# Subtracting the row maxima in attention with four 32-row tiles of the TensorE array instead of 64-row tiles

## The chip, the cores and the metric

The kernel runs on one core of one Trainium2 chip. The metric is the time of one execution in microseconds (us), as the median of several runs. A profile of one execution goes with it.

## The reference

The program is a transformer block: a layernorm, an attention layer with rotary positions, and a gated feed-forward layer whose inputs are rounded to blockwise FP4. The change is in the attention alone:

```
scores = einsum('bhid,bhjd->bhij', qr, kr) * 64**-0.5
probs  = softmax(scores, axis=-1)
out    = einsum('bhij,bhjd->bhid', probs, v)
```

There are 4 batches of 1024 tokens, 16 heads of 64 channels. The softmax subtracts each query's largest score before the exponential.

## The kernel before

Everything is written out by hand in Bass: one program for each engine, which runs its instructions in order, with semaphores between the engines.

**Tiling.** Two heads make a pair, 8 pairs a batch, 32 pairs (P) in all. Head 0 of a pair lies in partitions 0 to 63, head 1 in 64 to 127. A pair has 16 steps: 2 chunks (c) of 512 queries, each against 8 tiles (jt) of 128 keys. The loop of a pair (`pair(P)`) goes through 8 step pairs d = 0 to 7, each with the steps 2d and 2d+1.

**A step's scores.** `scores` (L853) writes, for each head, the transposed scores of 128 keys by 512 queries to one PSUM bank, `st[step % 2][:, a]`; so two buffers st with two banks each. Queries and keys are split into a high and a low part (`heads`), and the product is made of three terms. A fourth term subtracts the row maxima: the stationary operand `one_rows` has ones in its first four rows of each head, and `max_rows` holds in those rows, for each block of 128 queries, the negated maxima and zeros elsewhere. Each term is a pair of matmuls with 64 rows, one for each head, in the two halves of the array. A step waits until the exponential of the step two before it has read its st.

**Exponential.** ScalarE (L449) turns each st (128x1024) into `probs`, a ring of 8. TensorE multiplies probs by v into `po` (L865, 128 rows by 64 columns of the array, `times_v`), one step pair behind the scores.

**Row maxima.** They are those of the high parts alone, for the pair that comes next. `max_scores` (L898) writes 128 queries by 512 keys of both heads to `mx`, of which there is one buffer; VectorE reduces it to `negmax` (L644, `row_maxima`) and only then may the next mx be written. Each step pair has two such units, one ahead of its scores and one behind. After eight of them VectorE gathers `maxcol` (L649), TensorE transposes it (L905, `max_transpose`, unit "B", at the end of d=2 and d=6) and VectorE spreads it, times `mask`, over `max_rows` (L658). `mask` is 1 where the row of a head belongs to the block of queries.

**The other work of a step pair** goes through one PSUM bank, `ms`: the projections of keys and queries (L888, unit "K", d=0 to 3, read by VectorE in L674 and L675), of v (L878, "V", d=4 and 5), the output projection (L923, "O", d=6 and 7), and the sums of the probabilities over the keys (L914, "S", 128 rows by 32 columns, d=1 and 5). VectorE also adds the first two tiles of probs (L666, `first_sum`) at d=1, 3, 5 and 6; GpSimd adds the rest.

**TensorE's order in a step pair** is thus: first mx, scores of step 2d, scores of step 2d+1, second mx, the K, V or O unit, po of the two steps before, and the B or S unit if there is one. Pairs 0 to 30 have mx in all step pairs; pair 31 has it at d=0 and d=1 only.

Of the kernel before, what the change touches and what calls it, by code (L numbers as in the profile page):

```python
# [8 lines left out]
F32 = mybir.dt.float32  # L9
F32R = mybir.dt.float32r  # L10
I32 = mybir.dt.int32
ALU = mybir.AluOpType
ACT = mybir.ActivationFunctionType
AX = mybir.AxisListType
# [3 lines left out]
HEADS, HD = 16, 64  # L18
# [9 lines left out]
JT = TOKENS // PART  # L28
CH = 512
RING = 8  # L30
STEPS = 2 * JT
HALF = TPB // 2
SETS = 3
FIRST_KEYS = 2
QUARTER = CH // 2
KSL = [(0, 128), (128, 128), (256, FFN - 256)]
GT = 4
# [8 lines left out]
def wait(engine, semaphore, value):  # L46

    if value > 0:
        engine.wait_ge(semaphore, value)
# [7 lines left out]
def block_program(nc, ctx, x_d, gamma_d, beta_d, wqkv_d, wout_d, bout_d, wg_d, wu_d, wd_d,  # L57
                  cos_d, sin_d, ident_d, sums_d, recips_d, out_d):
    def sb(name, shape, dt=F32):
        return ctx.enter_context(nc.sbuf_tensor(name, shape, dt))  # L60

    def sem(name):
        return ctx.enter_context(nc.semaphore(name))
# [6 lines left out]
    ident = sb("ident", [PART, PART])  # L70
# [14 lines left out]
    max_rows = sb("max_rows", [PART, TOKENS], F32R)  # L85
    one_rows = sb("one_rows", [PART, PART], F32R)
    mask = sb("mask", [PART, HALF])
    v = sb("v", [PART, 2, JT, PART])
    negmax = sb("negmax", [PART, 2, 2, HALF, 2])
    maxcol = sb("maxcol", [PART, 2, PART])  # L90
    probs = sb("probs", [PART, RING, 2, CH])
    first_sum = sb("first_sum", [PART, 2, 2, CH])
    psum_keys = sb("psum_keys", [PART, 2, 2, CH])
    sums = sb("sums_kept", [PART, 2, QUARTER])
    oT = sb("oT", [PART, 2, TOKENS])
# [34 lines left out]
    st = [ctx.enter_context(nc.psum_tensor(f"st{i}", [PART, 2, CH], F32)) for i in range(2)]  # L130
# [9 lines left out]
    const_done, one_rows_done = sem("const_done"), sem("one_rows_done")  # L140
# [8 lines left out]
    mask_done, key_part = sem("mask_done"), sem("key_part")  # L149
    maxcol_done = sem("maxcol_done")  # L150
    st_ps, exp_done, pv_ps, key_sum = sem("st_ps"), sem("exp_done"), sem("pv_ps"), sem("key_sum")
# [19 lines left out]
    def maxima_at(P, d, second):  # L171

        n = 2 * d + second - 4
        return (P + 1, n) if n >= 0 else (P, n + 16)
# [9 lines left out]
    def units_at(P, d):  # L184

        return [(kind, target(P, kind, u), u) for kind, u in UNITS[d] if 0 <= target(P, kind, u) < PAIRS]
# [5 lines left out]
    def read_out(engine, unit):  # L192

        engine.wait_ge(ms_free, order_of[unit] + 1)

    def keys_added(P, c):

        return (JT - FIRST_KEYS - 1) * (2 * P + c)

# [16 lines left out]
    def present(P):  # L216

        return 0 <= P < PAIRS
# [90 lines left out]
    def _(pool):  # L309
# [3 lines left out]
        nc.gpsimd.memset(w_raw[:, :], 0.0).then_inc(const_done, 1)  # L313

        pool.wait_ge(const_done, 1)
        for a in range(2):
            nc.gpsimd.memset(one_rows[HD * a:HD * a + HALF, :].bitcast(F32), 1.0).then_inc(one_rows_done, 1)
        pool.wait_ge(one_rows_done, 2)

        def add_step(P, i):  # L320
            c, jt = i // JT, i % JT
            if jt <= FIRST_KEYS:
                return
            wait(pool, exp_done, STEPS * P + i + 1)
            if jt == FIRST_KEYS + 1:
                if P > 0:
                    filled(pool, ("S", P - 1, c))
                first = probs[:, (STEPS * P + i - 1) % RING]
            else:
                pool.wait_ge(key_sum, keys_added(P, c) + jt - FIRST_KEYS - 1)  # L330
                first = psum_keys[:, c]
# [82 lines left out]
    def _(act):  # L414
# [24 lines left out]
        def exp(P, i):  # L439
            step_n = STEPS * P + i  # L440
            act.wait_ge(st_ps, step_n + 1)
            if step_n >= RING:
                act.wait_ge(pv_ps, step_n - RING + 1)
                old, c, jt = (step_n - RING) // STEPS, ((step_n - RING) // JT) % 2, (step_n - RING) % JT
                if jt < FIRST_KEYS:
                    act.wait_ge(key_part, 2 * (2 * old + c) + 2)
                else:
                    act.wait_ge(key_sum, keys_added(old, c) + max(jt - FIRST_KEYS, 1))
            nc.scalar.activation(probs[:, step_n % RING], st[step_n % 2][:, :], ACT.Exp, scale=SCALE)\  # L449
# [8 lines left out]
        def sum_copy(F, c):  # L458
            filled(act, ("S", F, c))
            wait(act, sums_out, 16 * (2 * F + c - 1))  # L460
            nc.scalar.activation(sums[:, c, :], ms[:, 0:QUARTER], ACT.Copy).then_inc(ms_free, 1)  # L461

# [72 lines left out]
    def _(dve):  # L535
# [86 lines left out]
        mean_and_rstd(ln_attention, TPB, TILES, True)  # L622
        normalise_x(TPB, TILES)
        dve.wait_ge(consts_in, 96)
        nc.vector.tensor_tensor(mask[:, :], ident[:, 0:HALF], ident[:, HD:HD + HALF], ALU.add).then_inc(mask_done, 1)
        dve.wait_ge(mask_done, 1)

        def quantise_weights():
# [17 lines left out]

        def max_columns(N, c):
            dve.wait_ge(mx_free, 16 * N + 8 * c + 8)
            nc.vector.tensor_reduce(maxcol[:, c].rearrange("p (a k) -> p a k", a=2)[:, :, 0:HALF], negmax[:, c], AX.X,  # L649
                                    ALU.min).then_inc(maxcol_done, 1)  # L650

        def spread_maxima(N, c):

# [145 lines left out]
    def _(pe):  # L799
        mm = nc.tensor.matmul  # L800
        pe.wait_ge(consts_in, 96)
        pe.wait_ge(const_done, 1)
        pe.wait_ge(one_rows_done, 2)
        def transpose_xn(b):
            for c in range(2):
                pe.wait_ge(xn_done, TPB * b + 4 * c + 4)
                wait(pe, xnT_done, 2 * b + c - 1)
                for t in range(4):
                    last = nc.tensor.transpose(halves[c][:, t * PART:(t + 1) * PART],
                                               xn[:, b * TPB + 4 * c + t, :],  # L810
                                               ident[:, :])
                last.then_inc(xnT_ps, 1)
# [22 lines left out]
        def bank(unit):  # L835

            wait(pe, ms_free, order_of[unit])

        def scores(P, i):
            c, jt, step_n = i // JT, i % JT, STEPS * P + i  # L840
            if i == 0:
                pe.wait_ge(lo_done, 2 * P + 2)
            if jt == 0:
                read_out(pe, ("B", P, c))
            wait(pe, exp_done, step_n - 1)
            (k_hi, k_lo), (q_hi, q_lo) = ([heads[:, P % SETS, s, part] for part in range(2)] for s in range(2))
            keys, queries = bass.ts(jt, PART), bass.ts(c, CH)
            terms = ((k_lo[:, keys], q_hi[:, queries]), (k_hi[:, keys], q_hi[:, queries]),
                     (k_hi[:, keys], q_lo[:, queries]), (one_rows[:, :], max_rows[:, queries]))
            for n, (stationary, moving) in enumerate(terms):  # L850
                for a in range(2):
                    rows = slice(HD * a, HD * a + HD)
                    last = mm(st[step_n % 2][:, a], stationary[rows], moving[rows], start=(n == 0), stop=(n == 3))  # L853
            last.then_inc(st_ps, 1)

        def times_v(step_n):
# [34 lines left out]
        def max_scores(N, u):  # L891
            t, half = u // 2, u % 2
            wait(pe, mx_free, 16 * N + u)
            if u == 0:
                pe.wait_ge(hi_done, 2 * N + 2)
            for a in range(2):
                rows = slice(HD * a, HD * a + HD)
                last = mm(mx[:, a, :], heads[rows, N % SETS, 1, 0, bass.ts(t, PART)],  # L898
                          heads[rows, N % SETS, 0, 0, bass.ts(half, CH)], start=True, stop=True)
            last.then_inc(mx_full, 1)  # L900

        def max_transpose(N, c):
            bank(("B", N, c))
            pe.wait_ge(maxcol_done, 2 * N + c + 1)
            nc.tensor.transpose(ms[:, 0:PART], maxcol[:, c, :], ident[:, :]).then_inc(ms_full, 1)  # L905

        def softmax_sums(F, c):
# [3 lines left out]
            for part in (first_sum, psum_keys):  # L911
                for j in range(4):
                    a, quarter = j // 2, bass.ts(j % 2, QUARTER)
                    last = mm(ms[32 * j:32 * j + 32, 0:QUARTER], ones[:, 0:32], part[:, c, a, quarter],  # L914
                              start=part is first_sum, stop=part is psum_keys)
# [10 lines left out]

        def pair(P):
            for d in range(JT):
                N, u = maxima_at(P, d, 0)
                if present(N):  # L930
                    max_scores(N, u)
                if present(P):
                    scores(P, 2 * d)
                    scores(P, 2 * d + 1)
                N, u = maxima_at(P, d, 1)
                if present(N):
                    max_scores(N, u)
                for kind, X, u in units_at(P, d):
                    if kind == "K":
                        project_kq(X, u)  # L940
                    if kind == "V":
                        project_v(X, u)
                    if kind == "O":
                        output_projection(X, u)
                for n in (STEPS * P + 2 * d - 2, STEPS * P + 2 * d - 1):
                    if 0 <= n < STEPS * PAIRS:
                        times_v(n)
                for kind, X, u in units_at(P, d):
                    if kind == "B":
                        max_transpose(X, u)  # L950
                    if kind == "S":
                        softmax_sums(X, u)
# [106 lines left out]
```

## Time and profile before

| | |
|---|---|
| median of 3 runs | 1789.6 us (1787.51 to 1791.94) |
| profiled execution | 1791.84 us |
| span of its profile | 1790.1 us |
| mean granted TensorE clock | 0.962 |
| TensorE matmuls busy | 1613.1 us (90%) |
| VectorE / ScalarE / GpSimd busy | 1217.2 / 701.8 / 1234.8 us |

The span goes from the first to the last instruction in the profile; PE is TensorE's matmuls and PEld its weight loads, which overlap them; DVE is VectorE, ACT ScalarE, POOL GpSimd. The recorded duration of a matmul covers its passage through the array, and matmuls overlap: what one costs in a row of them is the distance between starts. Two matmuls in different row groups of the array run side by side.

### The profile page before, as it was taken

What the parts mean: (1) busy time and instruction counts of PE and PEld (TensorE: products, weight loads), DVE (VectorE), ACT (ScalarE), POOL (GpSimd) and SP (SyncE); (2) the same over time, 40 slices, a digit from 0 to 9 for tenths busy, and PEclk for the clock granted to TensorE, in tenths of its full rate; (3) what the DMA queues carried; (4) which work ended last, traced back from release to release, by engine and by line L of the source; (5) the groups of instructions that cost most, each with busy time, mean ns of one, the idle gap of its engine ahead of it and who ended that gap; (6) DMA issues with size and microseconds to landing.
All of it is one profiled execution on the core that took longest, in us unless ns stands there. A gap on an engine that the chain in (4) does not pass through costs nothing.

```text
span 1790.1 us, 25976 instructions
## 1 busy us (share of the span) xinstructions
PE 1613.1 (90%) x10025; PEld 872.1 (49%) x10025; DVE 1217.2 (68%) x1589; ACT 701.8 (39%) x885; POOL 1234.8 (69%) x562
## 2 busy tenths in 40 slices
PE   2499999999999999999999999999999999962576
PEld 1245555555555555555555555555555555531355
DVE  6566666666666666666666666676666666657787
ACT  0134444444444444444444444444444444421122
POOL 1647777777777777777777777777777777551563
PEclk9789999999999999999999999999999999985788
DMA  3111111111111111111111111111111111000000
GB/s 106 35 33 43 38 41 29 39 43 42 42 32 42 42 43 43 41 37 42 43 43 43 42 40 40 38 31 41 43 42 35 38 42 38 15 15 7 6 18 24
DMA packets 69194, 67.12 MB, mean 37 GB/s; under 512 B 26512, under 2 KB 52432, under 8 KB 69072
## 3 DMA queue, kind: packets, MB, share of 16 engines
q1 hardware_dynamic: 69072, 65.46, 14.3%
q8 instruction: 80, 1.31, 0.3%
q14 instruction: 42, 0.34, 0.1%
HBM read 29.25 MB, written 2.62 MB: 18 GB/s over the span
## 4 chain that ended last, share of the span: by engine, by line
PE 81%; DVE 15%; POOL 2%; issue 1%; DMA 0%; ACT 0%; SPq 0%; DVEq 0%; POOLq 0%
PE po L865 26%; PE st L853 23%; PE mx L898 9%; PE ms L888 8%; PE ms L878 4%; PE ms L923 4%; PE ms L914 4%; DVE negmax L644 2%; DVE first_sum L666 2%; DVE max_rows L658 1%; PE ms L905 1%; DVE amax L588 1%; DVE kq L720 1%; PE st L1000 1%; PE mx L977 1%
## 5 line engine op out<-in xcount | busy, mean ns | idle before, releaser
L644 DVE TENSOR_REDUCE negmax<-mx 128x2 f32<-128x1024 f32 x512 | 625.6, 1222 | 417.6 <-PE mx L898 417.6
L449 ACT ACTIVATE probs<-st 128x1024 f32<-128x1024 f32 x512 | 498.0, 1024 | 574.0 <-PE st L853 574.0
L332 POOL TENSOR_TENSOR psum_keys<-psum_keys,probs 128x1024 f32<-128x1024 f32 x256 | 607.5, 2373 | 149.7 <-ACT probs L449 132.7
L865 PE MATMUL po<-probs,v 128*64 128x512 f32 x2048 | 495.7, 605 | 0.0
L853 PE MATMUL st<-heads 64*128 64x512 f32 x3072 | 440.0, 391 | 0.0
L853 PEld LDWEIGHTS st<-heads 64*128 64x128 f32 x3072 | 289.9, 185 | 58.6 <-issue 2.4
L898 PE MATMUL mx<-heads 64*128 64x512 f32 x1024 | 236.7, 458 | 42.6 <-DVE negmax L644 41.9
L865 PEld LDWEIGHTS po<-probs,v 128*64 128x64 f32 x2048 | 124.3, 136 | 256.1 <-issue 147.1
L332 POOL TENSOR_TENSOR psum_keys<-probs 128x1024 f32<-128x1024 f32 x64 | 151.6, 2369 | 121.1 <-ACT probs L449 121.1
L344 POOL TENSOR_TENSOR kq<-kq 128x1024 f32<-128x1024 f32 x64 | 152.2, 2378 | 76.6 <-DMA kq<-sin_part 76.6
L853 PE MATMUL st<-max_rows,one_rows 64*128 64x512 f32 x1024 | 202.0, 389 | 0.0
L898 PEld LDWEIGHTS mx<-heads 64*128 64x128 f32 x1024 | 97.2, 186 | 211.0 <-issue 124.5
L888 PE MATMUL ms<-xnT,wqkv 128*128 128x512 f32 x256 | 151.1, 673 | 19.6 <-DVE sin_part L675 17.5
L666 DVE TENSOR_REDUCE first_sum<-probs 128x512 f32<-128x1024 f32 x128 | 159.3, 1245 | 5.1 <-ACT probs L449 5.1
L339 POOL TENSOR_TENSOR oT<-oT,rsum 128x512 f32<-128x512 f32 x64 | 82.3, 1286 | 111.4 <-DMA rsum<-recips 111.2
L348 POOL TENSOR_TENSOR heads<-kq,heads 128x1024 fp32r<-128x1024 f32 x64 | 153.1, 2393 | 1.6 <-ACT heads L472 1.6
L853 PEld LDWEIGHTS st<-max_rows,one_rows 64*128 64x128 f32 x1024 | 96.9, 185 | 21.7
L674 DVE TENSOR_TENSOR kq<-ms,cos 128x512 f32<-128x512 f32 x128 | 87.6, 684 | 23.0 <-PE ms L888 15.9
L923 PE MATMUL ms<-wout,oT 128*128 128x128 f32 x512 | 75.9, 292 | 22.6 <-issue 20.7
L658 DVE TENSOR_TENSOR max_rows<-ms,mask 128x512 fp32r<-128x512 f32 x64 | 44.3, 692 | 70.6 <-PE ms L905 70.6
L675 DVE TENSOR_TENSOR sin_part<-ms,sin 128x512 f32<-128x512 f32 x128 | 87.2, 681 | 0.0
L461 ACT ACTIVATE sums_kept<-ms 128x256 f32<-128x256 f32 x64 | 24.6, 385 | 153.4 <-PE ms L914 153.4
(129 smaller groups left out, 1145.1 us busy)
## 6 DMA issues: line engine op xcount, KB each, us to landing
kq<-sin_part SPq DMA_DIRECT2D x256, 128.0 KB, 2.4
rsum<-recips SPq DMA_DIRECT2D x128, 128.0 KB, 2.9
wqkv<-in_L_attn_w_qkv_dram SPq DMA_DIRECT2D x32, 192.0 KB, 2.7
resid<-in_L_attn_x_dram SPq DMA_DIRECT2D x4, 512.0 KB, 6.1
wout<-in_L_attn_w_out_dram SPq DMA_DIRECT2D x32, 64.0 KB, 2.6
out_dram<-resid SPq DMA_DIRECT2D x8, 256.0 KB, 2.3
sums<-sums_kept SPq DMA_DIRECT2D x64, 4.0 KB
spread<-sums SPq DMA_DIRECT2D x64, 4.0 KB, 1.6
```

Source lines behind the costliest of these rows:

```text
L332: nc.gpsimd.tensor_tensor(psum_keys[:, c], first, probs[:, (STEPS * P + i) % RING], ALU.add)\
L344: nc.gpsimd.tensor_tensor(raw[s], raw[s], swp[s], ALU.add).then_inc(rotated, 1)
L348: nc.gpsimd.tensor_tensor(heads[:, L % SETS, s, 1], raw[s], heads[:, L % SETS, s, 0].bitcast(F32), ALU.subtract)\
L449: nc.scalar.activation(probs[:, step_n % RING], st[step_n % 2][:, :], ACT.Exp, scale=SCALE)\
L644: nc.vector.tensor_reduce(negmax[:, t // HALF, :, t % HALF, half], mx[:, :], AX.X, ALU.max, negate=True)\
L666: nc.vector.tensor_reduce(first_sum[:, c, a], probs[:, 0:FIRST_KEYS, a].rearrange("p r n -> p n r"), AX.X, ALU.add).then_inc(key_part, 1)
L674: nc.vector.tensor_tensor(raw[s][:, columns], ms[:, :], cos[:, columns], ALU.mult).then_inc(cos_done, 1)
L853: last = mm(st[step_n % 2][:, a], stationary[rows], moving[rows], start=(n == 0), stop=(n == 3))
L865: last = mm(po[HD * a:HD * a + HD, :], v[:, P % 2, jt, HD * a:HD * a + HD], probs[:, step_n % RING, a], start=(jt == 0), stop=(jt == JT - 1))
L888: mm(ms[:, :], wqkv[:, L % 2, 1 - s, :], batch(L)[:, bass.ts(c, CH)], start=True, stop=True)\
L898: last = mm(mx[:, a, :], heads[rows, N % SETS, 1, 0, bass.ts(t, PART)], heads[rows, N % SETS, 0, 0, bass.ts(half, CH)], start=True, stop=True)
L923: last = mm(ms[:, bass.ts(t, D)], oT[:, F % 2, bass.ts(HALF * u + t, PART)], wout[:, :], start=True, stop=True)
```

## The change

The term with the row maxima leaves `scores` and becomes the function `minus_maxima`, called once for a step pair, ahead of the first mx. It makes four matmuls of 32 rows each, in four row tiles of the array, one for each of the two steps and two heads, into the four st banks. They open the accumulation (`start=True`), and the three terms of `scores` add to it. `max_rows` and `one_rows` therefore hold each head's rows twice (partitions 0, 32, 64 and 96 on), `maxcol` is written by two reductions, and `mask` sums four blocks of the identity. The wait for st moves along: the four matmuls wait for the exponentials of both steps of the step pair before, and at the first tile of a chunk for `max_rows`.

```
+        for j in range(4):
+            nc.gpsimd.memset(one_rows[QUAD * j:QUAD * j + HALF, :].bitcast(F32), 1.0).then_inc(one_rows_done, 1)
...
+        nc.vector.tensor_reduce(mask[:, :], ident[:, :].rearrange("p (j q) -> p q j", j=4)[:, 0:HALF], AX.X, ALU.add)\
...
-            nc.vector.tensor_reduce(maxcol[:, c].rearrange("p (a k) -> p a k", a=2)[:, :, 0:HALF], negmax[:, c], AX.X,
-                                    ALU.min).then_inc(maxcol_done, 1)
+            for twin in range(2):
+                nc.vector.tensor_reduce(maxcol[:, c].rearrange("p (s a k) -> p s a k", s=2, a=2)[:, twin, :, 0:HALF],
+                                        negmax[:, c], AX.X, ALU.min).then_inc(maxcol_done, 1)
...
+        def minus_maxima(P, i):
+            c, step_n = i // JT, STEPS * P + i
+            if i % JT == 0:
+                read_out(pe, ("B", P, c))
+            wait(pe, exp_done, step_n)
+            for j in range(4):
+                rows = slice(QUAD * j, QUAD * j + QUAD)
+                mm(st[j // 2][:, j % 2], one_rows[rows, :], max_rows[rows, bass.ts(c, CH)], start=True, stop=False,
+                   tile_position=(QUAD * j, 0))
+
         def scores(P, i):
             c, jt, step_n = i // JT, i % JT, STEPS * P + i
             if i == 0:
                 pe.wait_ge(lo_done, 2 * P + 2)
-            if jt == 0:
-                read_out(pe, ("B", P, c))
-            wait(pe, exp_done, step_n - 1)
...
-                     (k_hi[:, keys], q_lo[:, queries]), (one_rows[:, :], max_rows[:, queries]))
+                     (k_hi[:, keys], q_lo[:, queries]))
...
-                    last = mm(st[step_n % 2][:, a], stationary[rows], moving[rows], start=(n == 0), stop=(n == 3))
+                    last = mm(st[step_n % 2][:, a], stationary[rows], moving[rows], start=False, stop=(n == 2))
...
-            pe.wait_ge(maxcol_done, 2 * N + c + 1)
+            pe.wait_ge(maxcol_done, 2 * (2 * N + c) + 2)
...
         def pair(P):
             for d in range(JT):
+                if present(P):
+                    minus_maxima(P, 2 * d)
```

## Rows read from the trace of the kernel before

**Rows 1.** The page: busy time of each engine, and the chain that ended last.
```profile
PE 1613.1 (90%) x10025; PEld 872.1 (49%) x10025; DVE 1217.2 (68%) x1589; ACT 701.8 (39%) x885; POOL 1234.8 (69%) x562
...
PE 81%; DVE 15%; POOL 2%; issue 1%; DMA 0%; ACT 0%; SPq 0%; DVEq 0%; POOLq 0%
```

**Rows 2.** Stretch with attention: length, busy us (instructions) by engine, clock, DMA.
```profile
126.00:1640.00 1514.00, 1451.06 (x9354) 768.81 (x9352) 1014.27 (x1212) 643.92 (x756) 1106.56 (x500) 0.99 0.15 38
```

**Rows 3.** Timeline of TensorE's matmuls, one step pair (d=1): start us, length us, instructions.
```profile
668.29 0.50 PE L898 MATMUL mx<-heads 64*128 64x512 f32 x2
668.63 0.86 PE L853 MATMUL st<-heads 64*128 64x512 f32 x6
669.33 0.39 PE L853 MATMUL st<-max_rows,one_rows 64*128 64x512 f32 x2
...
670.25 0.40 PE L853 MATMUL st<-max_rows,one_rows 64*128 64x512 f32 x2
670.49 0.40 PE L898 MATMUL mx<-heads 64*128 64x512 f32 x2
670.81 1.12 PE L888 MATMUL ms<-xnT,wqkv 128*128 128x512 f32 x2
671.87 1.94 PE L865 MATMUL po<-probs,v 128*64 128x512 f32 x8
673.74 0.64 PE L914 MATMUL ms<-first_sum,ones 128*32 128x256 f32 x8
...
674.74 0.50 PE L898 MATMUL mx<-heads 64*128 64x512 f32 x2
```

**Rows 4.** Timeline of the weight loads at the end of it (idle before, releaser).
```profile
673.74 0.16 PEld L914 LDWEIGHTS ms<-first_sum,ones 128*32 128x32 f32 x8 [0.81 <-DVE sin_part L675]
...
674.74 0.19 PEld L898 LDWEIGHTS mx<-heads 64*128 64x128 f32 x2 [0.41 <-issue]
674.84 0.65 PEld L853 LDWEIGHTS st<-heads 64*128 64x128 f32 x6
```

**Rows 5.** Timeline of all engines, from the end of d=6 to d=7.
```profile
703.22 0.33 PE L905 MATMUL ms<-ident,maxcol 128*128 128x128 f32 x1
...
703.48 0.51 PE L898 MATMUL mx<-heads 64*128 64x512 f32 x2
...
703.59 0.69 DVE L658 TENSOR_TENSOR max_rows<-ms,mask 128x512 fp32r<-128x512 f32 x1 [1.39 <-PE ms L905]
...
704.20 1.25 DVE L666 TENSOR_REDUCE first_sum<-probs 128x512 f32<-128x1024 f32 x1
...
705.37 1.21 DVE L644 TENSOR_REDUCE negmax<-mx 128x2 f32<-128x1024 f32 x1
...
706.63 0.19 PEld L898 LDWEIGHTS mx<-heads 64*128 64x128 f32 x2 [1.24 <-DVE negmax L644]
...
707.07 0.41 PEld L923 LDWEIGHTS ms<-wout,oT 128*128 128x128 f32 x3 [0.25 <-issue]
```

**Rows 6.** Timeline of VectorE in the step pair of rows 3.
```profile
668.83 1.23 DVE L644 TENSOR_REDUCE negmax<-mx 128x2 f32<-128x1024 f32 x1 [0.93 <-PE mx L898]
...
672.19 0.17 DVE L649 TENSOR_REDUCE maxcol<-negmax 128x8 f32<-128x16 f32 x1
672.30 0.69 DVE L674 TENSOR_TENSOR kq<-ms,cos 128x512 f32<-128x512 f32 x1
672.90 0.68 DVE L675 TENSOR_TENSOR sin_part<-ms,sin 128x512 f32<-128x512 f32 x1
```

**Rows 7.** Waits over the span: us in total, times, longest us.
```profile
PEld mx L898 <- DVE negmax L644: 66.6, 47, 8.6
```

**Rows 8.** Timeline at the start of d=4: the first mx and its reduction.
```profile
685.85 0.50 PE L898 MATMUL mx<-heads 64*128 64x512 f32 x2
...
686.63 1.17 DVE L644 TENSOR_REDUCE negmax<-mx 128x2 f32<-128x1024 f32 x1
```

**Rows 9.** Timeline of ScalarE in the step pair of rows 3.
```profile
669.76 1.95 ACT L449 ACTIVATE probs<-st 128x1024 f32<-128x1024 f32 x2 [0.75 <-PE st L853]
```

More of the change, by code:

```diff
@@ L34 @@
 FIRST_KEYS = 2
+QUAD = 32
 QUARTER = CH // 2
@@ L315, in _ @@
         pool.wait_ge(const_done, 1)
-        for a in range(2):
-            nc.gpsimd.memset(one_rows[HD * a:HD * a + HALF, :].bitcast(F32), 1.0).then_inc(one_rows_done, 1)
-        pool.wait_ge(one_rows_done, 2)
+        for j in range(4):
+            nc.gpsimd.memset(one_rows[QUAD * j:QUAD * j + HALF, :].bitcast(F32), 1.0).then_inc(one_rows_done, 1)
+        pool.wait_ge(one_rows_done, 4)
         def add_step(P, i):
@@ L624, in _ @@
         dve.wait_ge(consts_in, 96)
-        nc.vector.tensor_tensor(mask[:, :], ident[:, 0:HALF], ident[:, HD:HD + HALF], ALU.add).then_inc(mask_done, 1)
+        nc.vector.tensor_reduce(mask[:, :], ident[:, :].rearrange("p (j q) -> p q j", j=4)[:, 0:HALF], AX.X, ALU.add)\
+          .then_inc(mask_done, 1)
         dve.wait_ge(mask_done, 1)
@@ L802, in _ @@
         pe.wait_ge(const_done, 1)
-        pe.wait_ge(one_rows_done, 2)
+        pe.wait_ge(one_rows_done, 4)
         def transpose_xn(b):
```

## The prediction

> **What bounds the kernel now.** I read the page's busy times first [rows 1]: TensorE's matmuls fill 90% of the span, VectorE 68%, ScalarE 39%, GpSimd 69%. The chain that ended last agrees, 81% TensorE and 15% VectorE. The stretches [rows 2] say where: from 126 to 1640 us, which is nearly all of the attention, matmuls cover 1451.06 of 1514 us at the full clock (0.99). So a microsecond taken off TensorE's queue counts there, unless VectorE turns out to stand right behind it. That needs one step pair at close range.
>
> The timeline of TensorE shows one step pair, d=1, whole [rows 3]. Pairs of 64-row products that follow each other start 0.23 us apart: the eight of two steps run from 668.63 to 670.49, 1.86 us. Where the shape of the array tile changes, it is dearer. The first pair of mx starts at 668.29 and the next pair only at 668.63, 0.34 instead of 0.23. The weight-load rows [rows 4] say why. Inside one shape the next weights load while the last products stream (674.84, 0.10 after the mx products start at 674.74). After a change of shape the loads begin only when the stream before is through: the idle of 0.41 us ahead of the mx loads at 674.74 is such a change, and the products then have to wait for those loads. The purest case is in [rows 5]: the mx pair at 706.63 came as the first and last of its shape, and the next shape's loads start at 707.07, 0.44 later.
>
> VectorE must reduce the first mx before the second may be written, for there is one mx buffer. In [rows 6] the first reduction starts at 668.83, takes 1.23 and ends at 670.06. How soon TensorE could go on after that is in [rows 5]: reduction 705.37 + 1.21 = 706.58, loads at 706.63, so 0.05. Second mx's loads might thus start at 670.11; the products start at 670.49, so the loads start 0.23 ahead of them, at 670.26. The slack is 0.15 us. This is the row the whole forecast rests on. The waits say the same from the other side: TensorE's mx loads waited for a reduction 47 times in 512 [rows 7].
>
> **The change part by part.**
>
> *Taken away:* in each pair of steps the two max_rows pairs (669.33 and 670.25 in [rows 3]), 2 x 0.23 = 0.46 us. Both lie between the first and the second mx. There are 32 x 8 = 256 step pairs.
>
> *What of that arrives.* With 0.46 gone the second mx meets VectorE. First mx to start of reduction 668.83 - 668.29 = 0.54, reduction 1.23, release 0.05, and then the mx pair loads and streams by itself, 0.44 to the next shape: 2.26 us from first mx to the ms unit. Before it is 670.81 - 668.29 = 2.52. So only 0.26 of the 0.46 arrives; the rest turns into a wait for VectorE.
>
> *Added:* one group of four 32-row products, ahead of the first mx. No row of before shows 32-row tiles. The price has two parts. The group itself: four column tiles of 32 run side by side (eight products of L914 with 256 columns in 0.64 us, [rows 3]) and their loads too (eight in 0.16 us, [rows 4]), and two row tiles do; so I take four row tiles as one pass, as long as one pair. The change of shape behind it, from 32 to 64 rows: every change in the rows, of rows or of columns (po to sums, sums to mx, mx to ms, po to mx), makes the loads wait. So I take the price of a pair alone in its shape, 0.44. The entry into the group from po or ms costs what the entry into mx did, and that is already in the 0.44. Lower bound 0.23 (a pair inside its shape, no drain). Upper bound 0.67: the four run as two passes, 0.44 + 0.23. I take 0.44, the row nearest in kind.
>
> The Trainium skill, page "TensorEngine Tiling (Array Packing)", section "Key Properties", says that changing the tiling mode, and not just the tile, drains the TensorE. By that rule the group costs 0.44 and by a free change 0.23, which is rival A; the trace agrees with it for every change it holds. The skill's page "TensorE: Matmul & The Clock Gate", Part 3, gives a measured speedup of 3.07 for four row tiles of 32. By it an estimate of the group's pass is 4 x 0.23 / 3.07 = 0.30 instead of 0.23 us, and the sum would be 219 x 0.07 = 15 us higher, about the top of the forecast's own range. No row of before shows it.
>
> *The sum of one step pair:* 0.44 - 0.26 = +0.18 us. It holds where VectorE is ready for the first mx. At two of the others, d=3 and d=4, it is late by up to 0.3 us ([rows 8], d=4: mx until 685.85 + 0.50 = 686.35, reduction from 686.63); the 0.44 swallows that, and the same +0.18 comes out within some hundredths. At d=7 it doesn't hold: VectorE takes max_rows, first_sum and then the reduction in one chain that starts with the transposition at 703.22, and the second mx waits for it until 706.63 [rows 5]. The first mx ends at 703.48 + 0.51 = 703.99; 0.44 later is 704.43, still before 705.37. So at d=7 the group is hidden whole, and the removed pairs give nothing either: 0.
>
> *Total:* seven of eight step pairs at +0.18 in pairs 0 to 30, 217 x 0.18 = 39.1; d=0 and d=1 of pair 31, +0.36; its other six have no mx, and give 0.44 - 0.46 = -0.02 each. Sum +39 us.
>
> *The moved wait.* The group writes both st buffers, so it waits for the exponential of the step before it, not of the one before that; behind it in TensorE's queue stand mx and the scores. The two exponentials of this d run 669.76 to 671.71 [rows 9], the next group would start at 674.74: 3.0 us of cover, nothing. With po as the only work between (pair 31) the cover is still over half a microsecond by the same sum: scores, 1.94 of po, against two exponentials of 1.95. The wait for the max_rows moves ahead of one mx and was met a step pair or more ago: they are written at d=2 and d=6 (L658), used at d=4 and at the next d=0.
>
> *maxcol twice:* 64 more reductions of VectorE at 0.17 us, in a chain before the cos and sin products of d=1 (672.19 in [rows 6], next instruction 0.11 later). The sums' loads at 673.74 wait for the sin product, which ends at 672.90 + 0.68 = 673.58: 0.16 apart, 0.05 of it release. That covers 0.11; between 0 and 0.06 x 32 = 2 us is left. I take 0. The mask's reduction and four memsets instead of two are at the start, behind other work: under 1 us.
>
> The profiled execution has a span of 1790.1 us and a time of 1791.8; the median of the runs is 1789.6. +39 on the span is +2.2%, which on the median is 1828.6; I say 1829.
>
> **The rivals.**
>
> *A. No drain between 32 and 64 rows.* The group costs 0.23 and mx then streams behind it as a pair within its shape. One step pair: mx starts 0.34 after the old place, reduction 0.43 after that (670.49 to 670.92), 1.23, 0.05, 0.44: 2.49 against 2.52, so -0.03. Times 219, -6 us: 1784, at the edge of no change. For it: nothing in the rows excludes it, since they hold no 32-row tile. Against it: all changes that they do hold drain. It decides from a price of the group of about 0.25 down; there the sign turns.
>
> *B. The group is dearer:* two passes, or slow writes to four banks at once. +0.23 at 219 places is +50 more, 1879. d=7 still hides it (704.66 before 705.37).
>
> *C. The plain ledger.* Two pairs go, one group of the same length comes, and VectorE isn't in the way: 256 x -0.23 = -59 us, 1731. It needs no drain and a reduction that ends 0.3 us sooner; the 0.15 of slack speaks against it.
>
> *D. A cheap drain.* The change costs 0.1 instead of 0.44 - 0.23 = 0.21, say because only the rows of the array are regrouped: the group is 0.34, a step pair 0.08 longer, 217 x 0.08 = +17, 1807.
>
> **How the numbers follow.** Forecast (drain, one pass): 0.68, own range 1815 to 1845. A: 0.13. B: 0.08. C: 0.03. D: 0.08. 0.3% of the median is 5 us, about what a measurement of this kernel tells from no change. Half of A falls within that bound and the rest is faster; with C that is 0.10 faster and 0.08 same (small mishaps included); the forecast, B and D are slower, 0.82. The range takes in A and D on the low side and leaves out B and C: 1782 to 1845.
>
> **What the profile after would show.** Right: loads of mx some 0.44 us after those of the group; the second mx's loads 0.05 after the end of a reduction at nearly all d, with the times that TensorE waited for negmax risen from 47 loads to over 200; a step pair 0.18 longer at all d but 7; the 1024 matmuls on max_rows still 1024, of 32 rows, starting a few ns apart in fours. Wrong: mx loads that start while the group streams (A); the fourth product of a group starting 0.2 or more after the first (B); the second mx free of waits (C). Also wrong would be waits of the group for probs, which I priced at nothing.

## The result, and the profile after

| | before | changed |
|---|---|---|
| median | 1790.45 us (4 runs, 1787.51 to 1791.94) | 1830.13 us (4 runs, 1829.2 to 1831.61) |
| span of the profile | 1790.1 us | 1829.0 us |
| TensorE matmuls busy | 1613.1 us | 1643.8 us |
| TensorE weight loads busy | 872.1 us | 819.3 us |

The change makes the kernel slower, by a ratio of 1.0224 (95% interval 1.0207 to 1.0242), 39.7 us. The forecast was 1829 us.

The page still shows TensorE busy for 90% of a span that is longer. A reader could be misled here: the number of matmuls is the same, and in every step pair two passes of the array have become one, yet the busy time is larger. The clock is not the reason: it was 0.99 in the attention stretch before [rows 2] and is 1.00 in the same stretch after, which is the last line below.

```profile
span 1829.0 us, 26041 instructions
...
PE 1643.8 (90%) x10025; PEld 819.3 (45%) x10025; DVE 1229.2 (67%) x1653; ACT 700.1 (38%) x885; POOL 1234.7 (68%) x564
...
PE 81%; DVE 15%; issue 1%; POOL 1%; DMA 0%; ACT 0%; SPq 0%; DVEq 0%; POOLq 0%
...
126.00:1640.00 1514.00, 1482.42 (x9328) 717.69 (x9324) 994.45 (x1206) 639.51 (x751) 1103.15 (x497) 1.00 0.15 38
```

The timeline of the same step pair as in [rows 3], of the changed kernel: start us, length us, instructions. L849 is the new group, L908 mx, L863 the scores, L898 the K unit.

```profile
682.69 0.51 PE L849 MATMUL st<-max_rows,one_rows 32*128 32x512 f32 x4
683.13 0.50 PE L908 MATMUL mx<-heads 64*128 64x512 f32 x2
683.47 1.56 PE L863 MATMUL st<-heads 64*128 64x512 f32 x12
684.96 0.50 PE L908 MATMUL mx<-heads 64*128 64x512 f32 x2
685.39 1.13 PE L898 MATMUL ms<-xnT,wqkv 128*128 128x512 f32 x2
686.45 1.94 PE L875 MATMUL po<-probs,v 128*64 128x512 f32 x8
...
689.31 0.51 PE L849 MATMUL st<-max_rows,one_rows 32*128 32x512 f32 x4
```

Its weight loads, and what ended the idle time before them (compare [rows 4]):

```profile
682.69 0.19 PEld L849 LDWEIGHTS st<-max_rows,one_rows 32*128 32x128 f32 x4 [0.81 <-issue]
683.13 0.19 PEld L908 LDWEIGHTS mx<-heads 64*128 64x128 f32 x2 [0.24 <-issue]
683.24 1.37 PEld L863 LDWEIGHTS st<-heads 64*128 64x128 f32 x12
684.96 0.19 PEld L908 LDWEIGHTS mx<-heads 64*128 64x128 f32 x2 [0.35 <-DVE negmax L646]
```

VectorE in the same stretch (compare [rows 6]):

```profile
683.68 1.23 DVE L646 TENSOR_REDUCE negmax<-mx 128x2 f32<-128x1024 f32 x1 [1.38 <-PE mx L908]
685.50 1.23 DVE L646 TENSOR_REDUCE negmax<-mx 128x2 f32<-128x1024 f32 x1 [0.60 <-PE mx L908]
686.76 0.24 DVE L652 TENSOR_REDUCE maxcol<-negmax 128x8 f32<-128x16 f32 x2
```

Both terms of the forecast can be read off. The loads of mx start at 683.13, 0.44 after those of the group at 682.69: the loads did not run beside the group's products, as they do inside one shape (683.24, 0.11 after 683.13). The reduction runs from 683.68 to 684.91, the loads of the second mx start at 684.96, 0.05 later. The loads of the six score pairs start at 683.24, take 1.37 and had ended at 684.61; the row of the second mx names negmax as what ended its 0.35 of idle. First mx to K unit is 685.39 - 683.13 = 2.26, as worked out. Group to K unit is 2.70, against 2.52 before. On the page the group counts as busy in full, for its row (682.69 to 683.20) reaches past the start of mx at 683.13: that is where the larger busy time comes from.

This one step pair stands for the others. Over pairs 0 to 30 of the two traces, the median time from the first instruction of a step pair (the first mx before, the group after) to the unit behind the second mx is 2.49 to 2.52 us before and 2.68 to 2.70 after at d=0 to 6, and 3.59 in both at d=7. What follows in a step pair takes the same time in both, and so, within 0.1 us, does what lies ahead of the first step pair and from d=7 of pair 30 to the end. All of the loss lies between the start of a step pair and that unit.

The waits over the whole span (compare [rows 7]):

```profile
PEld mx L908 <- DVE negmax L646: 143.6, 259, 10.1
```

259 times instead of 47. The count of before is too low as a measure of how close VectorE was, since a load that waited only a little is not in it. Loads of mx that start within 0.06 us of the end of the reduction that they need number 101 before, among them nearly all second ones of d=3, 4 and 7, and 256 after. The slack of 0.15 us that the forecast rests on was therefore there at five of the eight d only. And d=7 (compare [rows 5]): group, mx, VectorE's chain, second mx.

```profile
718.75 0.33 PE L915 MATMUL ms<-ident,maxcol 128*128 128x128 f32 x1
719.00 0.19 PEld L849 LDWEIGHTS st<-max_rows,one_rows 32*128 32x128 f32 x4
...
719.44 0.50 PE L908 MATMUL mx<-heads 64*128 64x512 f32 x2
...
720.88 1.22 DVE L646 TENSOR_REDUCE negmax<-mx 128x2 f32<-128x1024 f32 x1
...
722.16 0.19 PEld L908 LDWEIGHTS mx<-heads 64*128 64x128 f32 x2 [1.26 <-DVE negmax L646]
```

From the transposition to the second mx it takes 722.16 - 718.75 = 3.41 us, as before (706.63 - 703.22 = 3.41). The group is hidden there.

### The profile page after: what moved, and what is told of

It is laid out like the page before. It is cut to its first block, busy times and chain, and to the rows that moved or that the text cites. A ratio compares the mean times of both kernels' runs of the same rounds, so it can differ in the third digit from the quotient of the medians.

```text
span 1829.0 us, 26041 instructions
## 1 busy us (share of the span) xinstructions
PE 1643.8 (90%) x10025; PEld 819.3 (45%) x10025; DVE 1229.2 (67%) x1653; ACT 700.1 (38%) x885; POOL 1234.7 (68%) x564
## 4 chain that ended last, share of the span: by engine, by line
PE 81%; DVE 15%; issue 1%; POOL 1%; DMA 0%; ACT 0%; SPq 0%; DVEq 0%; POOLq 0%
PE po L875 26%; PE st L863 17%; PE mx L908 12%; PE ms L898 7%; PE st L849 5%; PE ms L888 4%; PE ms L933 4%; PE ms L924 3%; DVE negmax L646 2%; DVE first_sum L669 2%; DVE max_rows L661 1%; DVE amax L589 1%; PE ms L915 1%; DVE cos L590 1%; DVE kq L723 1%
## 5 line engine op out<-in xcount | busy, mean ns | idle before, releaser
L863 PE MATMUL st<-heads 64*128 64x512 f32 x3072 | 399.0, 391 | 0.0
L863 PEld LDWEIGHTS st<-heads 64*128 64x128 f32 x3072 | 291.8, 185 | 55.5 <-issue 1.5
L908 PE MATMUL mx<-heads 64*128 64x512 f32 x1024 | 259.2, 502 | 44.5 <-DVE negmax L646 44.4
L908 PEld LDWEIGHTS mx<-heads 64*128 64x128 f32 x1024 | 96.4, 185 | 206.3 <-DVE negmax L646 143.6
L898 PE MATMUL ms<-xnT,wqkv 128*128 128x512 f32 x256 | 149.3, 666 | 19.1 <-DVE sin_part L678 17.1
L849 PE MATMUL st<-max_rows,one_rows 32*128 32x512 f32 x1024 | 130.0, 497 | 0.6 <-ACT wdT L438 0.6
L849 PEld LDWEIGHTS st<-max_rows,one_rows 32*128 32x128 f32 x1024 | 49.0, 181 | 139.2 <-issue 104.6
L462 ACT ACTIVATE sums_kept<-ms 128x256 f32<-128x256 f32 x64 | 24.7, 386 | 152.3 <-PE ms L924 152.3
```

Of the source, the lines that this page charges most:

```text
L849: mm(st[j // 2][:, j % 2], one_rows[rows, :], max_rows[rows, bass.ts(c, CH)], start=True, stop=False, tile_position=(QUAD * j, 0))
L898: mm(ms[:, :], wqkv[:, L % 2, 1 - s, :], batch(L)[:, bass.ts(c, CH)], start=True, stop=True)\
```

## The experiments

The theory has three parts: (1) the group costs 0.44 us, 0.23 for its pass and 0.21 for the change of shape behind it; (2) of the 0.46 us that the removed pairs gave, VectorE's reduction of the one mx buffer lets only 0.26 through; (3) d=7 pays nothing, because it waits for VectorE anyway. The main rivals: the whole loss is the 32-row shape, or the whole loss is VectorE's wait. In these runs the kernel before had a median of 1791.3 us (first four) and 1791.6 us (last four). Differences between two experiments are between medians taken on one chip in one series. The changed kernel itself was measured in the series of the result, where before had 1790.45.

### e1_group_left_out: the changed kernel without the group

```
-            for j in range(4):
-                rows = slice(QUAD * j, QUAD * j + QUAD)
-                mm(st[j // 2][:, j % 2], one_rows[rows, :], max_rows[rows, bass.ts(c, CH)], start=True, stop=False,
-                   tile_position=(QUAD * j, 0))
...
-                    last = mm(st[step_n % 2][:, a], stationary[rows], moving[rows], start=False, stop=(n == 2))
+                    last = mm(st[step_n % 2][:, a], stationary[rows], moving[rows], start=(n == 0), stop=(n == 2))
```

> The changed kernel without its four 32-row products: the row maxima are not subtracted at all, the first of the three score terms opens the accumulation. My theory: the removed pairs give only 0.26 of their 0.46 us, since the second mx then stands at the reduction of the first; 219 x 0.26 = 57 us and six step pairs of 0.46 = 3 us below the kernel before, about 1731 us, and some 98 us below the changed kernel (219 x 0.44 plus 6 x 0.44). The waits of the mx loads for negmax stay at nearly all step pairs. Rival (VectorE is not in the way, the whole loss is the group): 256 x 0.46 = 118 us below before, about 1673 us, with few waits for negmax.

Measured: 1742.95 us, ratio 0.9733 (0.9719 to 0.9748): 48 us below before. That is far nearer to my 60 than to the 118 of the rival, and the mx loads waited for negmax 258 times: most of what the pairs cost cannot be had. This kernel leaves the subtraction of the maxima out. The rows of an ordinary step pair:

```profile
650.83 0.50 PE L904 MATMUL mx<-heads 64*128 64x512 f32 x2
...
652.65 0.19 PEld L904 LDWEIGHTS mx<-heads 64*128 64x128 f32 x2 [0.37 <-DVE negmax L646]
...
653.09 1.12 PE L894 MATMUL ms<-xnT,wqkv 128*128 128x512 f32 x2
```

First mx to K unit is 2.26 us, so 0.26 is gained. Most of the missing 12 us lies at d=3 and d=4. There VectorE comes late to the first mx [rows 8], and with no group to swallow that, little arrives. At d=3, and then at d=4:

```profile
662.45 0.50 PE L904 MATMUL mx<-heads 64*128 64x512 f32 x2
...
664.87 1.13 PE L894 MATMUL ms<-xnT,wqkv 128*128 128x512 f32 x2
...
667.79 0.49 PE L904 MATMUL mx<-heads 64*128 64x512 f32 x2
...
668.59 1.17 DVE L646 TENSOR_REDUCE negmax<-mx 128x2 f32<-128x1024 f32 x1
...
669.81 0.19 PEld L904 LDWEIGHTS mx<-heads 64*128 64x128 f32 x2 [0.57 <-DVE negmax L646]
...
670.25 0.71 PE L884 MATMUL ms<-wqkv,xnT 128*128 128x128 f32 x4
```

2.42 us at d=3 and 2.46 at d=4, where other step pairs now take 2.26. That is 0.36 us less gained in each of 31 pairs, 11 of the 12 us. My expectation for this run had forgotten what the prediction itself says of these two places.

### e2_pairs_of_64_first: the kernel before with its max_rows pairs ahead of mx, in 64 rows

```
+        def minus_maxima(P, i):
+            c, step_n = i // JT, STEPS * P + i
+            if i % JT == 0:
+                read_out(pe, ("B", P, c))
+            wait(pe, exp_done, step_n)
+            for s in range(2):
+                for a in range(2):
+                    rows = slice(HD * a, HD * a + HD)
+                    mm(st[s][:, a], one_rows[rows, :], max_rows[rows, bass.ts(c, CH)], start=True, stop=False)
...
+                if present(P):
+                    minus_maxima(P, 2 * d)
```

> The kernel before, with its two max_rows pairs (64 rows each, four matmuls for a step pair) moved ahead of the first mx, where they open the accumulation, with the same wait as in the changed kernel. No 32-row tile and no further change of shape. My theory: +0.46 ahead of the first mx and -0.26 behind it, +0.20 a step pair outside d=7, 219 x 0.20 = +44 us: about 1834 us. Rival (the 32-row shape is the whole loss): no work is added, so about 1790 us.

Measured: 1836.43 us, ratio 1.0254 (1.0237 to 1.0271), +45 us. The same matmuls in the same shapes, only moved to the other side of the first mx, cost as much as the whole change. So the 32-row shape is not needed for the loss. The rows:

```profile
684.93 0.73 PE L847 MATMUL st<-max_rows,one_rows 64*128 64x512 f32 x4
...
685.50 0.39 PE L905 MATMUL mx<-heads 64*128 64x512 f32 x2
...
687.21 0.19 PEld L905 LDWEIGHTS mx<-heads 64*128 64x128 f32 x2 [0.38 <-DVE negmax L644]
```

Here mx follows in the same shape (0.57 after the start of two pairs, 0.34 for the entry and 0.23 for the second), and the second mx again waits for negmax, 258 times in the whole span. The wait for the exponentials moved along here too, but it is not the cause: the max_rows loads of L847 had to wait for probs twice, 1.6 us together.

### e3_group_behind_first_mx: the changed kernel with the group between mx and the scores

```
-                if present(P):
-                    minus_maxima(P, 2 * d)
                 N, u = maxima_at(P, d, 0)
                 if present(N):
                     max_scores(N, u)
+                if present(P):
+                    minus_maxima(P, 2 * d)
```

> The changed kernel with the group of four between the first mx and the scores. Now there are two changes of shape (64 to 32 and 32 to 64 rows) and VectorE has its time. My theory: first mx alone 0.44, group 0.44, then 0.34 + 5 x 0.23 = 1.49 for the six score pairs to the second mx's start, 0.32 to the next unit: 2.69 against 2.52 of before, +0.17, nothing at d=7: about +37 us, 1827 us, with few waits for negmax. Rival A (a change between 32 and 64 rows is free): 1738 to 1745 us.

Measured: 1830.34 us, ratio 1.0217 (1.0202 to 1.0233), +39 us. Now VectorE has its time, and there are two more changes of shape than before instead of one; the loss is theirs:

```profile
682.76 0.49 PE L908 MATMUL mx<-heads 64*128 64x512 f32 x2
683.19 0.50 PE L849 MATMUL st<-max_rows,one_rows 32*128 32x512 f32 x4
...
683.62 1.67 PE L863 MATMUL st<-heads 64*128 64x512 f32 x12
684.91 0.19 PEld L908 LDWEIGHTS mx<-heads 64*128 64x128 f32 x2
685.13 0.40 PE L908 MATMUL mx<-heads 64*128 64x512 f32 x2
685.46 0.30 PEld L898 LDWEIGHTS ms<-xnT,wqkv 128*128 128x128 f32 x2 [0.36 <-issue]
```

Each of the two passes that end in a change, mx from 64 to 32 rows and the group from 32 back to 64, takes 0.43 from start to start. First mx to K unit is 2.70, as in the changed kernel, but made up of other terms; that the two losses agree is chance, and the 39 us here are not the price of the one change in the changed kernel. The mx loads waited for negmax 46 times in the whole span, as in the kernel before.

### e4_group_twice: the group made twice

```
-            for j in range(4):
+            for n, j in enumerate((0, 1, 2, 3, 0, 1, 2, 3)):
                 rows = slice(QUAD * j, QUAD * j + QUAD)
-                mm(st[j // 2][:, j % 2], one_rows[rows, :], max_rows[rows, bass.ts(c, CH)], start=True, stop=False,
+                mm(st[j // 2][:, j % 2], one_rows[rows, :], max_rows[rows, bass.ts(c, CH)], start=n < 4, stop=False,
```

> The changed kernel with its group of four products made twice (the maxima are subtracted twice), the second time accumulating. It prices a pass of four inside its shape: 0.23 if the four run side by side, so +0.23 at 217 places outside d=7 and at the eight of pair 31: about +51 us over the changed kernel, 1881 us. At d=7 it is still hidden. Rival B (four tiles are no single pass, and part of the 0.44 is that): +0.30 or more a group, 1897 us or more.

Measured: 1883.83 us, ratio 1.0518 (1.0503 to 1.0534), 54 us over the changed kernel of the result (51 expected).

```profile
702.66 0.74 PE L849 MATMUL st<-max_rows,one_rows 32*128 32x512 f32 x8
703.33 0.18 PEld L908 LDWEIGHTS mx<-heads 64*128 64x128 f32 x2 [0.37 <-issue]
```

Group to mx is 0.67 instead of 0.44. A pass of four row tiles inside its shape costs 0.23, like a pair; by subtraction the other 0.21 of the 0.44 is the change of shape. This rules out rival B.

### e5_before_half_reduction and e6_after_half_reduction: VectorE's reduction cut

Both kernels reduce only 256 of each head's 512 columns of mx, so the maxima are taken over half of the keys.

```
-            nc.vector.tensor_reduce(negmax[:, t // HALF, :, t % HALF, half], mx[:, :], AX.X, ALU.max, negate=True)\
+            nc.vector.tensor_reduce(negmax[:, t // HALF, :, t % HALF, half], mx[:, :, 0:QUARTER], AX.X, ALU.max, negate=True)\
```

> The kernel before with negmax reduced over 256 of each head's 512 columns of mx (half of the scores are left out of the maxima). It is the base for the next run. The reduction falls from 1.23 to about 0.62 us. Only d=7 waited for it: -0.6 x 31 = -19 us, about 1771 us.

Measured: 1769.07 us, ratio 0.9873 (0.9858 to 0.9887). The base is as expected within 2 us, in part by luck. The reduction takes 0.69 us, not 0.62. In the traces the span is 24.7 us shorter: 16 us of it are at d=7 (3.06 us instead of 3.59, 31 times), and nearly 6 lie ahead of the first step pair, where the expectation had none.

> The changed kernel with the same halved reduction. My theory: with VectorE out of the way all of the 0.46 arrives, against the 0.44 of the group: -0.02 a step pair against the run before this one, so -4 us, about 1767 us, and no waits for negmax outside d=7. Rival (VectorE's wait is no part of the loss): still 39 us above its base, about 1810 us.

Measured: 1766.06 us, ratio 0.9857 (0.9842 to 0.9871), 3 us below its base where 4 were expected; the two intervals overlap, so the two kernels are not told apart. The difference is far, though, from the 39.7 us by which the change is slower with the full reduction, and that is the result. The timeline of an ordinary step pair of e6:

```profile
655.84 0.51 PE L849 MATMUL st<-max_rows,one_rows 32*128 32x512 f32 x4
656.28 0.50 PE L908 MATMUL mx<-heads 64*128 64x512 f32 x2
656.83 0.69 DVE L646 TENSOR_REDUCE negmax<-mx 128x2 f32<-128x512 f32 x1 [1.46 <-PE mx L908]
...
657.77 0.20 PEld L908 LDWEIGHTS mx<-heads 64*128 64x128 f32 x2
658.00 0.41 PE L908 MATMUL mx<-heads 64*128 64x512 f32 x2
658.34 0.30 PEld L898 LDWEIGHTS ms<-xnT,wqkv 128*128 128x128 f32 x2 [0.36 <-issue]
```

The reduction is over at 657.52, the mx loads start at 657.77 without a wait, and group to K unit is 2.50 us against the 2.52 of [rows 3]. Over pairs 0 to 30 the second mx's loads start 0.25 to 0.26 us after the reduction's end at every d but 7. With VectorE out of the way, in this place and order, the change is worth next to nothing.

### e7_before_sum_first and e8_after_sum_first: the cover of d=7 taken away

On VectorE the first_sum of d=6 goes ahead of max_rows, into the 1.39 us in which VectorE waited for the transposition [rows 5].

```
                     if kind == "B":
+                        if d == 6 and present(P):
+                            first_keys(P, 1, 1)
                         spread_maxima(X, u)
...
-                if present(P) and d in (1, 3, 5, 6):
+                if present(P) and (d in (1, 3, 5) or d == 6 and P == PAIRS - 1):
                     first_keys(P, d // HALF, int(d in (3, 6)))
```

> The kernel before with VectorE's first_sum of d=6 ahead of max_rows, in the time in which VectorE waits for the transposition. It takes the cover away from d=7: there the second mx no longer waits about 1.0 us. 31 x 1.0 = -31 us, about 1759 us. Rival: the work comes back as a wait elsewhere (first_sum delays max_rows and the release of ms), 1780 to 1790 us.

Measured: 1757.13 us, ratio 0.981 (0.9796 to 0.9825), the fastest of the versions that leave nothing out. The rows of d=7:

```profile
689.50 0.33 PE L907 MATMUL ms<-ident,maxcol 128*128 128x128 f32 x1
...
690.47 1.22 DVE L644 TENSOR_REDUCE negmax<-mx 128x2 f32<-128x1024 f32 x1
...
691.96 0.40 PE L900 MATMUL mx<-heads 64*128 64x512 f32 x2
```

From the transposition to the second mx's products it is now 2.46 us instead of 3.41 (there the products start with the loads).

> The changed kernel with the same order on VectorE. My theory: d=7 was spared because its wait covered the group; with that wait gone it pays +0.18 like the others, so the distance to the run before this one grows from 39 to 39 + 31 x 0.18 = 45 us: about 1804 us. Rival (d=7 is spared for another reason): the distance stays 39 us.

Measured: 1802.11 us, ratio 1.0062 (1.0045 to 1.0079). The distance to e7 is 45.0 us, which was the number expected, where the change alone made 39.7. Now d=7 waits like the others:

```profile
709.15 0.50 PE L910 MATMUL mx<-heads 64*128 64x512 f32 x2
...
709.69 1.23 DVE L646 TENSOR_REDUCE negmax<-mx 128x2 f32<-128x1024 f32 x1 [0.18 <-PE mx L910]
...
710.97 0.19 PEld L910 LDWEIGHTS mx<-heads 64*128 64x128 f32 x2 [0.36 <-DVE negmax L646]
```

## Why the prediction was right

- **The removed pairs give 0.26, not 0.46.** Right in size, and by the mechanism named: 0.05 from a reduction's end to the next mx's loads, 259 such waits. The 0.26 is more than the slack of 0.15. The rest is on TensorE: before, the second mx's loads came at 670.25 by the trace, its products at 670.49 and the K unit at 670.81, 0.56 us behind the loads; after a wait the products start with the loads, and it takes 0.43 (684.96 to 685.39). e6 shows the other side: with a shorter reduction all of it arrives. That e2 loses as much without any new shape shows that the place of the work, ahead of the first mx, matters as much as its amount.
- **The group costs 0.44.** Right: 0.44 in the timeline after; e4 parts it into 0.23 for the pass and 0.21 for the change of shape. Rival A (no drain) and rival D (a cheap one) fall with it. The four products of a group start within 0.01 us of each other at all 256 places, which with e4 excludes rival B. The rule of the Trainium skill, page "TensorEngine Tiling (Array Packing)", section "Key Properties", that a change of tiling mode drains the TensorE, agrees with the trace for 64 to 32 rows and back: in e3 a lone pass takes 0.43 us in front of either change, against 0.23 inside a shape. The 3.07 times for four row tiles of the Trainium skill's page "TensorE: Matmul & The Clock Gate", Part 3, would have made the pass an estimated 0.30 us. Measured in e4 it is 0.23, as long as a pair of 64-row products: page and measurement differ, and the measurement decides.
- **d=7 pays nothing.** Right: 3.41 us before and after, and e8 pays once the cover is gone.
- **d=3 and d=4** swallow VectorE's lateness in the group. Right for the change: at both, the reduction now starts 0.54 us after the first mx, as elsewhere, instead of 0.72 and 0.79. e1, in which there is no group, shows that the lateness is real.
- **Moved wait and double maxcol at nothing.** The profile bears it out: the group's loads waited for probs twice in the whole span, 1.6 us together, which is no more than the 0.8 of idle that stands before a group anyway, and the pair of maxcol takes 0.24 us instead of 0.17 at d=1 and delays nothing that shows: the sums' loads come 1.86 us after po's start, as before (688.31 - 686.45, and 673.74 - 671.87 = 1.87).

```profile
  issue: 104.6, 160
...
  ACT probs L450: 1.6, 2
```

These rows are of line L849 in the trace after: what ended the idle time before the group, in us and times.

The sum came out at 39 us and was 39.7 (38.9 in the spans of the two profiles). It was made of figures rounded to 0.01 us, and 0.01 at 217 places is 2 us, so part of this closeness is luck.

The plain ledger, two pairs against one group of four (rival C, -59 us), fails twice over: on the change of shape (e3: +39 us with VectorE out of the way, from two changes) and on VectorE (e2: +45 us without a further change of shape). In the changed kernel neither alone makes the loss. With the drain but no wait the change is worth nothing (e6 against e5). The other combination, no drain with the wait, was not tried; the prediction's sum for it, 6 us faster (rival A), is argued and not shown.

## What to carry to other kernels

Before counting what a shorter stretch of one engine saves, look for the row of the other engine that lies between the same two instructions: here the reduction ended 0.15 us before it was needed, and only 0.26 of the 0.46 us could be had. A small matmul in a shape of its own cost its pass plus a change of shape here, 0.23 + 0.21 us, nearly the 0.46 of the two passes it replaced; packing two passes into one would need neighbours of its shape to pay, which no run here tried. And work moved from one side of a handover to the other, with nothing added to it, can cost as much as added work: 45 us in e2.

## What was not expected of the hardware

Halving the columns of VectorE's reduction did not halve its time: 1.23 us for 128x1024 and 0.69 us for 128x512, so by an estimate from these two lengths some 0.15 us of it doesn't shrink (2 x 0.69 - 1.23). Two maxcol reductions of 0.17 us each, one behind the other, took 0.24 us together. The 0.05 us from the end of VectorE's reduction to the start of the loads that waited for it hardly varied: 0.051 to 0.053 us at 256 places of the changed kernel.
